# Four stacked attention layers: two of four probability turns moved from TensorE to VectorE and DRAM, with a new order table

## What is computed

```
L0: x1 = LN(x  + attention(x, x, causal))            16 heads of 16   (attention 0)
    x2 = LN(x1 + attention(x1, ctx))                 16 heads of 16   (attention 1)
    x3 = LN(x2 + fc2(relu(fc1(x2))))
L1: h  = x3 + attention(rms(x3), rms(ctx), rope) Wo  16 heads of 64, 4 key heads (attention 2)
    x4 = h + down(silu(gate(rms h)) * up(rms h))     hidden 1024
L2: x5 = x4 + attention(LN(x4), LN(ctx)) Wo + bo     (attention 3)
L3: y  = LN(x5 + attention(x5, ctx, masked, clipped to 50) Wo + bo)   (attention 4)
```

## Time and profile before

| | |
|---|---|
| time, median of 3 runs | 4003.32 us (4002.51 to 4005.87) |
| span of the profiled execution | 3996.0 us; the page gives no other time of it |
| median above that span | 7.3 us |
| busy: TensorE, weight loads, VectorE, ScalarE, GpSimd | 99%, 86%, 73%, 67%, 31% |
| DMA | 69.65 MB, mean 17 GB/s |
| TensorE's granted clock, mean | 0.999 of full speed |

### The profile page before, as it was taken

How to read it: one execution, slowest core, us unless ns; L and a number is a source line. 1 busy time by engine, 2 the same in 40 slices (tenths; PEclk the granted TensorE clock), 3 DMA queues, 4 the chain that set the end, 5 groups by cost and what they waited for, 6 DMA issues and landing times.

```text
span 3996.0 us, 116007 instructions
## 1 busy us (share of the span) xinstructions
PE 3939.4 (99%) x44820; PEld 3452.9 (86%) x44820; DVE 2932.9 (73%) x10721; ACT 2676.8 (67%) x8449; POOL 1233.8 (31%) x2247
## 2 busy tenths in 40 slices
PE   7999999999999999999999999999999999999998
PEld 7888888888888888888888888888888888888886
DVE  4677777777777777777777777777777777777764
ACT  3676766776766766767767767667667667676663
POOL 1233333233232332333332332323323333323321
PEclk9999999999999999999999999999999999999999
DMA  3000000000000000000000000000000000000000
GB/s 146 5 15 18 10 18 18 10 18 17 10 18 17 10 18 16 12 18 10 18 18 10 17 18 10 18 18 10 18 17 11 18 10 18 18 10 18 18 3 5
DMA packets 66498, 69.65 MB, mean 17 GB/s; under 512 B 7456, under 2 KB 64800, under 8 KB 65056
## 3 DMA queue, kind: packets, MB, share of 16 engines
q1 hardware_dynamic: 65952, 62.25, 5.0%
HBM read 53.83 MB, written 8.39 MB: 16 GB/s over the span
## 4 chain that ended last, share of the span: by engine, by line
PE 89%; DVE 6%; ACT 2%; issue 1%; POOL 1%; DMA 0%; SPq 0%; DVEq 0%; POOLq 0%; ACTq 0%
PE gen_ps L513 54%; PE gen_ps L505 16%; PE gen_ps L635 6%; PE scores_ps L609 5%; PE gen_ps L647 3%; PE scores_ps L595 3%; PE scores_ps L602 2%; PE scores_ps L588 1%; ACT oT L747 1%; DVE wide L935 1%; DVE zn L980 1%; DVE v L1040 1%; DVE rdenm L977 1%; DVE res L1044 1%; DVE plainT L1043 1%
## 5 line engine op out<-in xcount | busy, mean ns | idle before, releaser
L513 PE MATMUL gen_ps<-actT,w_sb 128*128 128x128 f32 x10752 | 1345.7, 278 | 12.2 <-DMA w_sb<-weights_dram 8.3
L513 PEld LDWEIGHTS gen_ps<-actT,w_sb 128*128 128x128 f32 x10752 | 1261.4, 192 | 67.6 <-issue 47.4
L836 POOL TENSOR_TENSOR rstd<-ve,consts 128x1 f32<-128x1 f32 x448 | 283.4, 633 | 1421.7 <-DVE ve L987 842.1
L747 ACT ACTIVATE probT<-gen_ps 128x512 f32<-128x512 f32 x1024 | 577.2, 634 | 210.5 <-PE gen_ps L505 207.3
L781 ACT ACTIVATE prob<-scores_ps,negmax 128x128 f32<-128x128 f32 x2048 | 568.6, 417 | 199.0 <-DVE negmax L1025 198.9
L505 PE MATMUL gen_ps<-consts,prob 128*128 128x128 f32 x4096 | 598.3, 276 | 11.4 <-ACT prob L781 5.7
L505 PEld LDWEIGHTS gen_ps<-consts,prob 128*128 128x128 f32 x4096 | 467.4, 141 | 122.1 <-ACT prob L781 57.2
L513 PE MATMUL gen_ps<-w_sb,wide 128*128 128x256 f32 x2056 | 465.4, 379 | 0.9 <-DVE wide L1165 0.6
L513 PE MATMUL gen_ps<-w_sb,actT 128*128 128x256 f32 x1792 | 462.5, 381 | 2.7 <-ACT actT L747 2.1
L897 POOL TENSOR_SCALAR prob<-prob,rden 128x128 f32<-128x128 f32 x1024 | 366.7, 380 | 314.7 <-DVE rden L1098 314.7
L747 ACT ACTIVATE actT<-gen_ps 128x256 f32<-128x256 f32 (+1 forms) x512 | 238.8, 466 | 285.0 <-PE gen_ps L505 284.9
(11 more groups left out here) (118 smaller groups left out, 6085.0 us busy)
## 6 DMA issues: line engine op xcount, KB each, us to landing
actT<-xT_dram SPq DMA_DIRECT2D x64, 128.0 KB, 2.2
ctx_rms<-x_dram SPq DMA_DIRECT2D x64, 128.0 KB, 2.2
ctx<-ctx_dram SPq DMA_DIRECT2D x64, 128.0 KB, 2.2
ctxT<-ctxT_dram SPq DMA_DIRECT2D x64, 128.0 KB, 2.3
mask<-mask_dram SPq DMA_DIRECT2D x128, 64.0 KB, 2.1
out_dram<-res SPq DMA_DIRECT2D x64, 128.0 KB, 1.7
w_sb<-weights_dram SPq DMA_DIRECT2D x2, 2048.0 KB, 18.8
w_sb<-weights_dram SPq DMA_DIRECT2D x2, 1024.0 KB, 20.5
```

What stands on the lines that cost most here:

```text
L513: last = nc.tensor.matmul(ps, lhsT(c), rhs(c), start=(c == 0), stop=(c == chunks - 1))
L747: release(nc.scalar.activation(dst, take(act, name, b)[:, 0:width], ACT.Copy), name, b)
L836: nc.gpsimd.tensor_tensor(dst, src, const("expo")[:, 0:width], ALU.pow)\
```

## The change

1. The turns of attentions 0 and 2 (BY_VECTOR) leave TensorE and ScalarE. VectorE transposes 32 x 32 blocks of a unit into the new buffer `turned`; SyncE sends 256 KB to DRAM and fetches them back into probT in another order, in pieces of 512 bytes. The products read probT in runs of 32 columns.
2. Six slots (G = 6) for the batch's rows; `wide` has 2 slots, plainT and v16 4, qT its own buffer with 3, probT 2 slots of a whole attention. The waits for free slots follow.
3. Moved to ScalarE: the scaling of two rms norms and of one layer norm (with a bias nb4 from VectorE), the spread queries of attentions 0 and 1, and the copy of the attention 2 values.
4. The additions of epsilon move from VectorE to GpSimd, one small operation ahead of each power; the 1/D of the mean square moves into ScalarE's scale.
5. PERIOD 69.73 becomes 55.62, and all times of LIFE are new; SyncE's transfers have a place in it too. Banks are given by the planned time at which they are read (count_plan). BESIDE and BANK_LATE are gone.

```diff
-G = 4
+G = 6
+N_WIDE = 2
+N_CTXT = 3
+N_Q = 3
+N_V = 4
+N_K = 4
+N_PT = 2
+BY_VECTOR = (0, 2)
+N_T = 4
+N_FAR = 4
-PERIOD = 69.731652
+PERIOD = 55.615500
...
+    ("scores", 0, 0, {"PE": 19.781}),
+    ("turn", 0, 3, {"DVE": 34.753}),
+    ("values", 0, 0, {"ACT": 40.654, "PE": 36.013}),
...
+    ("x2T", 1, 0, {"ACT": 116.396, "PE": 115.184}),
+    ("h", 1, 0, {"ACT": 119.074, "PE": 119.101}),
+    ("z", 1, 0, {"DVE": 122.223, "PE": 119.903, "POOL": 175.811}),
...
+    ("scores", 2, 0, {"PE": 158.901}),
+    ("turn", 2, 3, {"DVE": 172.216}),
+    ("out2", 2, 0, {"ACT": 179.056, "PE": 186.249}),
...
+    ("scores", 3, 0, {"PE": 226.223}),
+    ("soft", 3, 0, {"ACT": 228.759, "DVE": 228.939}),
+    ("turn", 3, 2, {"ACT": 233.630, "PE": 240.975}),
...
 def count_plan(events):
-    uses = [(use, b) for name, a, b, u in events if (use := bank_use(name, a, u))]
-    return {use: (k % N_GEN, k // N_GEN + 1) for k, use in enumerate(uses)}
...
+            j = min(range(N_GEN), key=lambda j: free[j])
+            free[j] = max(PERIOD * b + starts[name, a, u][e] for e in engines)
...
+            def weights_of(a, b, u, k):
+                part = probT[:, TURN_OF[a, b] % N_PT, u, :, :]
+                if a not in BY_VECTOR:
+                    return part[:, k, :]
+                return part.rearrange("p q (k j) -> p q k j", j=32)[:, :, k, :]
...
+            def turn(a, b, u):
+                n = turned_unit(a, b, u)
+                if a == 2:
+                    dve.wait_ge(sem("normed"), U * b + u + 1)
+                else:
+                    dve.wait_ge(sem("exp_done"), unit(a, b, u) + 1)
+                if n >= N_T:
+                    dve.wait_ge(sent_sem(n), 16 * (n // N_T))
+                nc.vector.transpose(turned[:, n % N_T, :, :, :].rearrange("p t k j -> p k t j"),
+                                    prob[:, u, :, :].rearrange("p k (i t) -> p k t i", t=R)).then_inc(sem("turned"), 1)
...
+                def send(a, b, u):
+                    n = turned_unit(a, b, u)
+                    k = T_OF[a, b]
+                    sp.wait_ge(sem("turned"), n + 1)
+                    if k >= N_FAR:
+                        fetched(sp, *TURNED[k - N_FAR], u)
+                    sp.dma_start(turned_d[n % (U * N_FAR)].rearrange("q (i t) x -> (q i) (t x)", t=R),
+                                 turned[:, n % N_T, :, :, :].rearrange("p t k j -> p (t k j)"))\
+                        .then_inc(sent_sem(n), 16)
+                def take_back(a, b, u):
+                    n = turned_unit(a, b, u)
+                    sp.wait_ge(sent_sem(n), 16 * (n // N_T + 1))
+                    probT_read(sp, a, b)
+                    sp.dma_start(probT[:, TURN_OF[a, b] % N_PT, u, :, :],
+                                 turned_d[n % (U * N_FAR)].rearrange("q t x -> t q x")).then_inc(fetched_sem(a, b, u), 16)
...
-            def rsqrt(src, dst, wait, signal, b, width=1):
+            def rsqrt(src, dst, eps, wait, signal, b):
                 pool.wait_ge(sem(wait), b + 1)
-                nc.gpsimd.tensor_tensor(dst, src, const("expo")[:, 0:width], ALU.pow)\
-                    .then_inc(sem(signal), 1)
+                nc.gpsimd.tensor_scalar(dst, src, eps, 0.0, ALU.add, ALU.add).then_inc(sem("padded"), 1)
+                padded[0] += 1
+                pool.wait_ge(sem("padded"), padded[0])
+                nc.gpsimd.tensor_tensor(dst, dst, const("expo")[:, 0:1], ALU.pow).then_inc(sem(signal), 1)
...
+                elif name == "queries":
+                    for e in range(2):
+                        ins = nc.scalar.activation(qT[:, Q_PLACE[a, b] % N_Q, :, e, :], ps, ACT.Copy,
+                                                   scale=const("parityq")[:, e:e + 1])
+                elif name == "rms_norm":
+                    nc.scalar.activation(zn[:, g, :], xs[:, g, :], ACT.Copy, scale=rstd[:, g, 0:1])\
+                        .then_inc(sem(signal), 1)
+                elif name == "norm_x4":
+                    nc.scalar.activation(zn[:, g, :], xs[:, g, :], ACT.Identity, bias=nb[:, g:g + 1],
+                                         scale=rstd[:, g, 0:1]).then_inc(sem("n4"), 1)
```

More of the change, by code:

```diff
@@ new lines @@
+    ("keys", 1, 0, {"ACT": 58.437, "PE": 58.839}),
+    ("queries", 1, 0, {"ACT": 62.592, "DVE": 64.263, "PE": 59.916}),
+    ("first_row", 1, 0, {"DVE": 76.647, "PE": 75.397}),
+    ("scores", 1, 0, {"PE": 81.128}),
+    ("send", 0, 1, {"SP": 85.472}),
+    ("soft", 1, 0, {"ACT": 89.717, "DVE": 85.682}),
+    ("fetch", 0, 1, {"SP": 86.673}),
+    ("send", 0, 0, {"SP": 86.849}),
+    ("send", 0, 2, {"SP": 86.872}),
+    ("soft", 1, 1, {"ACT": 89.734, "DVE": 88.178}),
+    ("fetch", 0, 2, {"SP": 88.634}),
@@ L261 @@
-N_GEN = 4
-BANK_LATE = {"t32", "t33"}
-def count_plan(events):
-    uses = [(use, b) for name, a, b, u in events if (use := bank_use(name, a, u))]
-    return {use: (k % N_GEN, k // N_GEN + 1) for k, use in enumerate(uses)}
+N_GEN = 4
+READERS = {"queries": {0: ("ACT", "DVE"), 1: ("ACT", "DVE"), 3: ("DVE",), 4: ("DVE",)}, "keys": "ACT", "first_row": "DVE",
+           "values": "ACT", "attended": "DVE", "tr": "ACT", "x2T": "ACT", "h": "ACT", "z": "DVE", "q2": "DVE",
+           "kv2": ("DVE", "ACT"), "out2": "ACT", "turn": "ACT", "o2": "DVE", "nT": "ACT", "gate": "DVE", "up": "DVE", "down": "DVE",
+           "zT": "ACT", "o": "DVE", "betas": "DVE", "bo": "DVE"}
@@ new lines, in readers_of @@
+def readers_of(name, a):
+    engines = READERS[name][a] if name == "queries" else READERS[name]
+    return (engines,) if isinstance(engines, str) else engines
+def count_plan(events):
+    starts = {(name, a, u): times for name, a, u, times in LIFE}
+    starts.update({(name, 0, u): times for name, u, times in ONCE})
+    free, full, read, out = [-1e9] * N_GEN, [0] * N_GEN, [0] * N_GEN, {}
+    for name, a, b, u in events:
+        use = bank_use(name, a, u)
+        if use:
+            engines = readers_of(name, a)
+            j = min(range(N_GEN), key=lambda j: free[j])
+            free[j] = max(PERIOD * b + starts[name, a, u][e] for e in engines)
+            before = read[j]
+            full[j] += 1
+            read[j] += len(engines)
+            out[use, b] = (j, full[j], read[j], before)
+    return out
@@ L1235, in _ @@
+                for g in range(G):
+                    sp.wait_ge(stored_sem(g), 16 * len(range(g, B, G)))
             @block.tensor
```

674 lines of the change are left out of this document (356 added, 318 removed).

## The result

The changed kernel takes **4173.3 us** (median of 4 runs, 4164.77 to 4185.77) where the kernel before takes 4003.54 on the same chip: a ratio of 1.0425, 95% interval 1.0404 to 1.0446. It is 4.2% slower. The prediction was 3862 us, 3.5% faster, with a range of 3745 to 4000.

A forecast was written before the change was run, and what follows sets the result against it. TensorE, busy 99%, was taken to bound the kernel: 60.75 - 3.4 = 57.3, plus 0.8 net new wait, 58.1 us a batch. 63 x 58.1 + 195 for the edges = 3855, plus 7.3 gives 3862 us, range 3745 to 4000.

The forecast's parts named there:

- Where the new wait is: ScalarE's row of steps after the third attention holds TensorE 1.9 us between z and scores(0); 0.8 net a batch.
- TensorE, 3.4 us per batch less and a floor of 57.3: Eight transpose groups of 0.43 us leave TensorE, so a batch comes no faster than 60.75 - 3.4 = 57.3 us.
- VectorE 45.8 us: VectorE's work per batch: loses 5.1 us, gains eight transposes at 0.65 and a bias of 0.15, stays at 45.8.
- ScalarE 40.4 us: ScalarE's work per batch: eight copies go, copies for queries and values and three norms come, from 41.8 to 40.4 us.
- The queue: SyncE's 23 transfers a batch take 10 us of 58 to issue; even at 2 us per fetch it has room.
- Is the round trip covered?: A 5.8 us trip is hidden with 4 us to spare in the first attention, just in time in the third.
- The wait for h: TensorE could start z at 13.7 us after the third attention's scores but waits for ScalarE's h until 14.7.
- Fill and drain, 195: Edges of 168.7 us gain 9 for two uncovered round trips and 20 for slower clock without fillers; 195 taken.
- B: VectorE's transposes cost double, 1.36 us, delaying soft(3,0) by 2.9: 61.0 us a batch, 4045 us; chance 0.10.
- A: No new wait, exponentials and turns overlap better: 57.0 us a batch in its sum, 3773 us; chance 0.22.
- C: VectorE and GpSimd share a port, each turn(2, u) waits 0.36 us, 1.4 a batch: 3950 us; chance 0.12.
- D: Round trip takes 9 us instead of 5.8 and holds the third attention's out2, 1.5 a batch: 3957 us; chance 0.08.

The follow-up runs named there:

- the pair of searched kernels: Changed kernel with VectorE turning no attention's probabilities, or both attentions', start times searched for each: 4026.33 us and 3857.46 us.
- the searched order: Changed kernel, VectorE turning both attentions, same instructions and buffers, only the table's start times searched for few TensorE waits: 3857.46 us, ratio 0.9636.
- the one with none: Changed kernel with TensorE turning all four attentions, no round trip, start times searched the same way: 4026.33 us, ratio 1.0056.
- the two named steps: Changed kernel with the attention 2 values' copy ahead of the fourth norm on ScalarE and context statistics two periods later on VectorE: 4028.03 us, ratio 1.0059.

## Why the prediction was wrong

It was 311 us off: 63 x (62.40 - 58.1) = 271 from the period, 247 - 195 = 52 from the edges, less 12 because the changed kernel's profiled span lies 4.7 us above the median, where before it lay 7.3 below.

**The step that failed** is the end of "Where the new wait is": "Behind that it runs without a wait in my walk through gate, up, values and down; the next scores(2) waits 0.2 for the key rotation." Measured: 2.4 us there, each batch, and 0.7 us of slow clock with it. Of the 4.3 us by which a batch was longer than forecast, these are 2.9. The wait for L1266's bank adds 0.5, and the wait for h is 0.4 longer than in the walk; how the rest divides is not known. The walk had followed TensorE and the turns, but not the two queues that feed the rotation: on ScalarE the values' copy behind norm_x4, on VectorE nb4 behind the MLP. The diff held both: it moved the copy from VectorE to ScalarE, and the norm as well, and made one wait in a row of both. Moving this copy alone ahead took 91 us off the changed kernel. That moved entry should have been followed past each neighbour.

Point by point:

- TensorE, 3.4 us per batch less and a floor of 57.3: right. 3.32 by the pair of searched kernels; with a good order the whole period is 57.85. The sum of 58.1 a batch was right for this design, and wrong for this table: 3862 was forecast, 3857 is what the same steps take in another order. That it agrees so closely is partly luck, as terms below were off both ways.
- VectorE 45.8 us: it is 3146.9/64 = 49.2 (the terms of the prediction add to 46.1). The turn, taken at 0.65 between 0.435 and 1.36, measures 1.11. In the order of the change this was worth 46 us, in the searched one 26.
- ScalarE 40.4 us: 40.6. GpSimd's small addition takes 0.22 us instead of 0.38; nothing hung on it.
- The queue, "SyncE has room": right on the average and wrong in place. Bandwidth: 24.6% of 4178/64 is 16.1 us of each batch (15 more on 3 were forecast); sends land in 2.8 us and fetches in 3.4, not 2.0 and 2.9. But the loads stand in order behind waits for turns and sends, and VectorE's wait for the context, 3.0 us where the timeline shows one, was in no step of mine; taken away alone it was worth 51 us.
- "Is the round trip covered?": right for the steady part, even at 0.46 us more per turn and 1.3 us more per trip. It is not covered in batch 0, as said, but costs there more than the 9 us of the sum.
- The wait for h: right in kind and place; 1.4 us in the rows where the walk had 1.0 of 1.9.
- Fill and drain, 195 (its terms 168.7 + 9 + 20 add to 198): 247 in this order, 209 in the searched. The clock's part was sized right (22 where the kernel before loses it). The round trips' part was not: without them 170, with both 209, so 39 where 9 was forecast, though the two orders differ too. The first 276 us of the kernel with both and of the one with none:

```profile
0.00:276.00 276.00, 201.40 (x2224) 175.48 (x2225) 180.60 (x650) 139.18 (x450) 73.33 (x157) 0.86 0.36 124
```

```profile
0.00:276.00 276.00, 235.15 (x2525) 203.38 (x2526) 158.86 (x645) 166.16 (x514) 76.36 (x157) 0.93 0.16 58
```

  With both, TensorE is idle for 74.6 us of them, with none for 40.9, and the granted clock is 0.86 and 0.93. Of the idle time 24.9 us are the wait for batch 0's trip, and 10 of these go when the weights are loaded later. The first store comes no later for it (276.2 and 292.6 us); so what is missing is work of the batches behind. How the rest divides is not shown.

The rivals. B, a turn at 1.36 us, came near in price, and just under its own point of decision (1.2); but its mechanism was not what made the kernel slow, since with turns of 0.64 it stays slow. A, no new wait, is what the searched order nearly reaches: 57.85, not 57.0. C and D did not happen. For C: a turn at 2047.74 us lies wholly beside GpSimd's normalisation and takes what all take,

```profile
2045.96 3.14 POOL L994 TENSOR_SCALAR prob<-prob,rden 128x128 f32<-128x128 f32 x8 [0.50 <-DVE rden L1212]
2047.74 1.11 DVE L1135 STREAM_TRANSPOSE turned<-prob 128x512 f32<-128x512 f32 x1
```

and the longest of 512 turns is 1.152 us. The 192 turns that overlap this normalisation take 1.117 us in the median, the 259 beside no GpSimd operation 1.114.

By the Trainium skill ("SBUF — State Buffer", section "SBUF: two separate sides") the shared port pair is locked for a whole instruction where VectorE runs in a two-port mode, or where it reads two inputs in SBUF beside a GpSimd operation that reads SBUF too. A turn has one input, so the rule would hold for it only in a two-port mode; whether it runs in one no row tells, but the turns show no lock. The last step of a layer norm has two: it takes 0.70 us at 2034.83, beside a GpSimd operation of 1.24 us from 2034.71, and 0.48 at 1993.68, as in the earlier trace rows. It is slowed, but by its row it ends at 2035.53, ahead of the GpSimd operation's 2035.95, so it did not wait for the whole of it; and the 63 such steps that overlap the normalisation take 0.485 us, as if alone. So the 0.72 us that the prediction set beside this rule belong to one kind of GpSimd operation, and not to the one beside the turns.

For D: none of TensorE's waits for the fetch comes in each batch.

What stays open: how the 2.1 us of period that the order cost beyond the two named steps (59.99 to 57.85) divide over the single entries; the search changed all at once.

## What to carry to other kernels

When a step is moved to another engine, list the steps it now stands behind there and what each of them waits for, and then who waits for the moved step on a third engine: here a 0.37 us copy behind a late norm cost 1.5 us a batch. Judge a design only in an order fitted to it: the same instructions were 4.2% slower or 3.6% faster than before. Which durations stood behind the changed kernel's table is not on record; what is shown is that a search with the measured ones found a much better one. Look in the queue of loads for anything that stands behind a wait for computed data, and issue or use it at another place.

## What the hardware showed that I had not expected

- VectorE's block transpose of float32 takes 1.115 us for 128x512 and 0.641 for 128x256: 1.85 ns for each further element of a row, where other VectorE operations of this kernel with a source in SBUF take 0.435 us for the same 512. The Trainium skill ("Vector Engine (DVE) Microarchitecture Reference", section "3.8 The reshape front-end and per-opcode configuration") says that a transpose is pipelined to one element per cycle and lane; the trace has two and a half times the plain operation's time for this type and these strides, and no run here tells which of the two is the reason.
- A wait of TensorE of 2.43 to 2.46 us was followed by products at full length in 23 batches and by products up to 1.7 times as long in 14 (granted clock 0.59 where one was looked at), so its length alone does not decide. On the average a batch had 0.7 us more of TensorE's time than without this wait (57.7 against 57.05), over a quarter on top of the wait; waits of 1.4 and 1.5 us in each batch, in the run with the values' copy ahead, left the clock at 1.00.
- The last step of a layer norm on VectorE (two inputs in SBUF) takes 0.70 us beside GpSimd's 1.24 us operation (L957) and 0.485 beside its normalisation (L994), so what a GpSimd operation costs VectorE depends on which one it is.
- Twice the turns cost 0.8 us of period for each us of VectorE, turns of half the heads gave back 0.2 in the same order: what a shorter step is worth could not be read from what a longer one costs.
